# Attention probabilities turned in 32x32 blocks on VectorE and moved by DMA, in place of transposes on TensorE

## The reference

```
# layer 0: graph attention, F1 = 256
h     = x @ W                                   # 512 x 256
e     = leaky_relu(h @ a[0] + (h @ a[1]).T, 0.2)
alpha = softmax(where(adj, e, -1e9))
x     = layernorm(x + concat([alpha @ h, h]))

# layer 1: 8 heads of 64
q, k, v = x @ Wq.T + bq, x @ Wk.T + bk, x @ Wv.T + bv
attn    = softmax(where(adj == 0, -inf, q @ k.T / 8))     # per head, 512 x 512
x       = layernorm(x + (attn @ v) @ Wo.T + bo)
```

## Time and profile before

| | us |
|---|---|
| median of 3 runs | 3468.46 (3467.27 to 3468.61) |
| the profiled execution | 3468.5 |
| its span, first to last instruction | 3466.6 |
| TensorE busy in the span | 3412.3 |
| VectorE busy | 2688.1 |
| ScalarE busy | 2510.2 |
| GpSimd busy | 1616.8 |

### The profile page before, as it was taken

One profiled execution on the slowest core, in us unless ns is written; L12 is line 12 of the kernel. 1 busy time (PEld: TensorE's weight loads), 2 busy tenths in 40 slices (PEclk: granted clock), 3 DMA queues, 4 the chain that ended last, 5 costly groups with the idle time before them and its releaser, 6 DMA issues.

```text
span 3466.6 us, 65791 instructions
## 1 busy us (share of the span) xinstructions
PE 3412.3 (98%) x23168; PEld 2903.8 (84%) x23168; DVE 2688.1 (78%) x7607; ACT 2510.2 (72%) x5382; POOL 1616.8 (47%) x1542
## 2 busy tenths in 40 slices
PE   6999999999999999999999999999999999999998
PEld 5888888888888888888888888888888888888886
DVE  5787777877777877778777778777787777877776
ACT  4776777776777767777777777677777777777775
POOL 2544454445454444544454544445444454444443
PEclk8999999999999999999999999999999999999999
DMA  3000011000111010110001110001100011100100
GB/s 128 19 22 28 25 38 38 31 26 22 34 38 38 20 31 25 37 38 31 26 21 36 38 35 22 26 31 38 38 25 32 19 38 37 32 25 25 31 13 25
DMA packets 59652, 111.19 MB, mean 32 GB/s; under 512 B 6720, under 2 KB 7488, under 8 KB 59328
## 3 DMA queue, kind: packets, MB, share of 16 engines
q1 hardware_dynamic: 59328, 106.99, 9.6%
HBM read 73.41 MB, written 33.55 MB: 31 GB/s over the span
## 4 chain that ended last, share of the span: by engine, by line
PE 97%; DVE 1%; ACT 1%; issue 0%; DMA 0%; POOL 0%; SPq 0%; ACTq 0%; DVEq 0%; POOLq 0%
PE R_bank L541 47%; PE O_bank L629 14%; PE T_bank L613 14%; PE S_bank L603 13%; PE L_bank L541 5%; PE L_bank L532 3%; PE L_bank L556 0%; DMA prob<-WkT 0%; POOL turned L985 0%; DVE prob L900 0%; PE O_bank L541 0%; DMA alpha<-a 0%; ACT tokens L674 0%; DVE n_wide L946 0%; ACT prob L734 0%
## 5 line engine op out<-in xcount | busy, mean ns | idle before, releaser
L965 POOL TENSOR_TENSOR prob<-prob,rsum 128x512 f32<-128x512 f32 x1024 | 1059.5, 1041 | 1309.3 <-DVE rsum L906 1307.4
L734 ACT ACTIVATE prob<-prob,negmax 128x512 f32<-128x512 f32 x1024 | 739.6, 722 | 323.3 <-DVE negmax L900 314.9
L659 ACT ACTIVATE probT<-T_bank 128x512 fp32r<-128x512 f32 x1024 | 579.0, 594 | 220.8 <-PE T_bank L613 214.6
L900 DVE CUSTOM_DVE_ANT_0 prob<-S_bank,mask 128x512 f32<-128x512 f32 x1024 | 695.5, 679 | 2.2 <-PE S_bank L603 1.1
L794 DVE TENSOR_TENSOR probT<-T_bank,probT 128x512 fp32r<-128x512 f32 x1024 | 675.9, 683 | 5.1 <-ACT probT L659 3.1
L613 PE MATMUL T_bank<-ident,prob 128*128 128x128 f32 x4096 | 597.7, 276 | 3.1 <-DVE probT L794 3.1
L629 PE MATMUL O_bank<-probT,v_st 128*128 128x256 f32 x4096 | 586.6, 288 | 2.8 <-DVE probT L794 2.8
L906 DVE RECIPROCAL rsum<-psum_row 128x1 f32<-128x1 f32 x1024 | 164.9, 161 | 542.7 <-PE S_bank L603 303.4
L613 PEld LDWEIGHTS T_bank<-ident,prob 128*128 128x128 f32 x4096 | 459.0, 141 | 106.1 <-issue 93.8
L629 PEld LDWEIGHTS O_bank<-probT,v_st 128*128 128x128 f32 x4096 | 522.2, 190 | 21.5 <-issue 11.5
L603 PE MATMUL S_bank<-qk_pair 64*128 64x512 f32 x3072 | 494.1, 426 | 2.5 <-DVE negmax L900 2.2
(11 more groups left out here) (84 smaller groups left out, 4374.0 us busy)
## 6 DMA issues: line engine op xcount, KB each, us to landing
tokens<-xT SPq DMA_DIRECT2D x128, 256.0 KB, 3.0
tokens<-x SPq DMA_DIRECT2D x128, 256.0 KB, 2.7
out<-tokens SPq DMA_DIRECT2D x128, 256.0 KB, 2.1
tokens<-adj SPq DMA_DIRECT2D x1, 1024.0 KB, 6.5
tokens<-WqT SPq DMA_DIRECT2D x1, 1024.0 KB, 5.5
prob<-WkT SPq DMA_DIRECT2D x1, 1024.0 KB, 7.9
tokens<-WvT SPq DMA_DIRECT2D x1, 1024.0 KB, 6.5
prob<-WoT SPq DMA_DIRECT2D x1, 1024.0 KB, 5.0
```

Of the source, the lines that this page charges most:

```text
L659: act.activation(dst, src, ACT.Copy).then_inc(done, 1)
L734: act.activation(prob[:, slot, :], prob[:, slot, :], ACT.Exp, bias=negmax[:, slot:slot + 1], scale=-1.0, accum_out=psum_row[:, slot:slot + ...
L900: dve.tensor_tensor_reduce(prob[:, slot, :], S_bank[s % 2][:, :], mask[:, s % 8 // 2, :], -SCALE, HUGE, ALU.add, ALU.min, negmax[:, slot:s ...
L965: pool.tensor_tensor(prob[:, slot, :], prob[:, slot, :], rsum[:, slot:slot + 1].to_broadcast([P, N]), ALU.mult).then_inc(p_norm, 1)
```

## The change

The probabilities are no longer transposed on TensorE.

- **Phases.** Four tiles (two row tiles of both heads) are a phase, eight a graph. Tiles 0, 1 and 2 of a phase are normalised on GpSimd (`norm`, now 24 a graph), tile 3 on ScalarE (`anorm`, 8).
- **`vt`** (32 a graph): VectorE's block transpose turns each 32x32 block of a normalised tile of `prob` within itself and writes it to `blocked`, which holds two phases, so that for one block row the pieces of four tiles lie side by side.
- **`mv`** (32 a graph): SyncE moves them, four transfers each, 128 a graph. Each takes 32 partitions of 2 KB to the 32 partitions where they belong in `turned_lo_prob` (two phases). 16 transfers make a phase; the first waits for the phase's fourth turn.
- **`hi` and `lo`**: ScalarE copies a quarter of a phase, 128x512, from `turned_lo_prob` to `turned_hi_prob` (one phase only); GpSimd, not VectorE, subtracts it in place. The first `hi` of a phase waits for both weighs of the phase before.
- **`weigh`** waits for all four `lo` of its phase and reads 256 queries as four runs of 64. `lows` and `sum` put the columns back in order (`by_row_block`).
- **Banks.** The two `T_bank`s go; there are three `S_bank`s, used in turn by tile, and two `L_bank`s. `scores` waits for one tile less to be reduced. N's result is read by ScalarE straight from `L_bank`; `n_wide` and its copy on VectorE go.
- **Buffers.** `turned`, `alpha` and `qk_pair` hold one tile, one tile and one pair where they held two. The reciprocal (`inv`) is a step of its own in VectorE's list.
- All lists of steps are written anew.

The diff, cut:

```diff
+    "scores N k1",
+    "weigh weigh C0",
+    "scores O0 scores",
+    "O1 scores O2",
+    "C1 weigh weigh",
+    "scores O3 q2",
+    "k2 D0 scores",
+    "weigh weigh scores",
+    "C2 D1 W0",
+    "W1 scores W2",
+    "W3 C3 D2",
+    "A3 weigh weigh",
+    "scores D3 q3",
+    "k3 weigh weigh",
+    "E0 E1 scores",
+    "scores V0 V1",
+    "E2 scores E3",
+    "weigh weigh scores",
+    "B0 q4 k4",
+    "B1 weigh weigh",
+    "scores V2 scores",
+    "B2 scores V3",
+    "weigh weigh B3",
+    "q1",
...
+    "norm pair norm",
+    "lo norm lo",
+    "lo lo norm",
+    "norm lo lo",
+    "lo norm lo",
+    "yrs norm norm",
+    "lo lo lo",
+    "norm lo norm",
+    "norm pair lo",
+    "norm lo lo",
+    "lo lrs norm",
+    "norm A0 lo",
+    "lo lo norm",
+    "lo bo0 norm",
+    "norm pair lo",
+    "lo norm A1",
+    "lo lo norm",
+    "norm A2 lo",
+    "lo lo norm",
+    "lo A3 norm",
+    "norm pair lo",
+    "norm lo lo",
+    "lo bo1 bo2",
+    "bo3",
...
+UNITS = {"scores": (16, 3), "reduce": (32, 6), "inv": (32, 5), "exp": (32, 6), "norm": (24, 4), "vt": (32, 4), "mv": (32, 1), "hi": (32, 0), "lo": (32, 0), "weigh": (16, -2), "lows": (8, -1), "sum": (8, -1), "pair": (4, -1), "anorm": (8, 1)}
+ENDING = """weigh weigh sum O0 lows pair evO0 evO1 O1 yst0 yst1 evO2 yst2 fin0 evO3 fin1 fin2 yst3 O2 O3 fin3 yrs"""
...
-        turned = sb("turned", [P, 2, 2, C, P], F32R)
+        turned = sb("turned", [P, 2, C, P], F32R)
...
-        alpha = sb("alpha", [P, 2, N])
+        alpha = sb("alpha", [P, N])
...
-        qk_pair = sb("qk_pair", [P, 2, 4, N], F32R)
+        qk_pair = sb("qk_pair", [P, 4, N], F32R)
...
-        probT = sb("probT", [P, HALVES, 2, T, 2 * P], F32R)
+        blocked = sb("blocked", [P, 2, 4, T, 4, BLK])
+        turned_lo_prob = sb("turned_lo_prob", [P, 2, 4, T, P], F32R)
+        turned_hi_prob = sb("turned_hi_prob", [P, 4, T, P], F32R)
...
-        S_bank = [bank(f"S_bank{i}") for i in range(2)]
-        T_bank = [bank(f"T_bank{i}") for i in range(2)]
+        S_bank = [bank(f"S_bank{i}") for i in range(3)]
         O_bank = bank("O_bank")
         R_bank = [bank(f"R_bank{i}") for i in range(2)]
-        L_bank = bank("L_bank")
+        L_bank = [bank(f"L_bank{i}") for i in range(2)]
...
+        def score_bank(R, s):
+
+            return S_bank[(32 * R.k + s) % 3]
+
+        def moved(R, ph, a):
+
+            return p_moved[ph % 2][a], 64 * ((8 * R.k + ph) // 2 + 1)
+
+        def prob_tile(s):
+
+            return prob[:, s % SLOTS, :]
 
         def o_cols(w):
 
             return slice(2 * P * w, 2 * P * (w + 1))
+
+        def by_row_block(half):
+
+            return half.rearrange("p (t a i) -> p a t i", t=2, a=4)
...
+            def move_probs(R, m):
+                ph, a = m // 4, m % 4
+                if a == 0:
+                    sp.wait_ge(p_turned, R.n(32, 4 * ph + 4))
+                own = slice(BLK * a, BLK * (a + 1))
+                for d in range(4):
+                    sp.dma_start(turned_lo_prob[BLK * d:BLK * (d + 1), ph % 2, a, :, :].rearrange("p c x -> p (c x)").bitcast(F32),
+                                 blocked[own, ph % 2, d, :, :, :].rearrange("p c j i -> p (c j i)")).then_inc(moved(R, ph, a)[0], 16)
...
-                if due(R.n(32, 2 * u)):
-                    pe.wait_ge(s_red, R.n(32, 2 * u))
-                qk = qk_pair[:, pair % 2, :, :]
+                if due(R.n(32, 2 * u - 1)):
+                    pe.wait_ge(s_red, R.n(32, 2 * u - 1))
                 for j, (qp, kp) in enumerate(PARTS):
                     for w in range(2):
                         own, _ = rows_of(w)
-                        last = pe.matmul(S_bank[w][:, :], qk[own, qp, t * P:(t + 1) * P], qk[own, 2 + kp, :],
-                                         start=j == 0, stop=j == 2)
+                        last = pe.matmul(score_bank(R, 2 * u + w)[:, :], qk_pair[own, qp, t * P:(t + 1) * P],
+                                         qk_pair[own, 2 + kp, :], start=j == 0, stop=j == 2)
...
-            def turn_probs(R, s):
-                pe.wait_ge(p_norm, R.n(32, s + 1))
-                if due(R.n(16, s // 2)):
-                    pe.wait_ge(t_lo[s % 2], R.n(16, s // 2))
-                for c in range(T):
-                    last = pe.transpose(T_bank[s % 2][:, c * P:(c + 1) * P], prob[:, s % SLOTS, c * P:(c + 1) * P],
-                                        ident[:, :])
-                last.then_inc(t_mm, 1)
-
             def weigh(R, g):
-                pair, half, w = half_of(g)
-
-                pe.wait_ge(t_lo[w], R.n(16, 4 * pair + 2 * half + 2))
+                ph, w = g // 2, g % 2
+
+                pe.wait_ge(p_lo, R.n(32, 4 * ph + 4))
...
+                    probs = (turned_hi_prob[:, :, c, DH * w:DH * (w + 1)],
+                             turned_lo_prob[:, ph % 2, :, c, DH * w:DH * (w + 1)])[s]
+                    last = pe.matmul(O_bank[:, o_cols(w)], v_st[:, c, (2 * (ph // 2) + w) % HEADS, :], probs,
+                                     start=(c, s) == todo[0], stop=(c, s) == todo[-1])
...
-                if due(R.n(32, 8 * (pair - 1))):
-                    act.wait_ge(s_mm, R.n(32, 8 * (pair - 1)))
+                if due(R.n(32, 8 * pair)):
+                    act.wait_ge(s_mm, R.n(32, 8 * pair))
...
-            def probs_hi(R, s):
-                pair, t, w = tile_of(s)
-                g = 4 * pair + t // 2 * 2 + w
-                if t % 2 == 0 and due(R.n(16, g - HALVES + 1)):
-                    act.wait_ge(pv_mm, R.n(16, g - HALVES + 1))
-                act.wait_ge(t_mm, R.n(32, s + 1))
-                split_hi(probT[:, half_buffer(R, g), HI, :, (t % 2) * P:(t % 2 + 1) * P],
-                         T_bank[s % 2][:, :].rearrange("p (c q) -> p c q", c=T), t_hi)
+            def probs_hi(R, m):
+                ph, a = m // 4, m % 4
+                if a == 0 and due(R.n(16, 2 * ph)):
+                    act.wait_ge(pv_mm, R.n(16, 2 * ph))
+                act.wait_ge(*moved(R, ph, a))
+                split_hi(turned_hi_prob[:, a, :, :], turned_lo_prob[:, ph % 2, a, :, :].bitcast(F32), p_hi)
+
+            def normalise_last(R, ph):
+                slot = (4 * ph + 3) % SLOTS
+                act.wait_ge(p_inv, R.n(32, 4 * ph + 4))
+                act.activation(prob[:, slot, :], prob[:, slot, :], ACT.Copy,
+                               scale=rsum[:, slot:slot + 1]).then_inc(p_norm_act, 1)
...
+                    dve.wait_ge(p_turned, R.n(32, s - SLOTS + 1))
...
-            def probs_lo(R, s):
-                pair, t, w = tile_of(s)
-                buf = half_buffer(R, 4 * pair + t // 2 * 2 + w)
-                dve.wait_ge(t_hi, R.n(32, s + 1))
-                cols = slice((t % 2) * P, (t % 2 + 1) * P)
-                split_lo(probT[:, buf, LO, :, cols], T_bank[s % 2][:, :].rearrange("p (c q) -> p c q", c=T),
-                         probT[:, buf, HI, :, cols], t_lo[w])
+            def turn_blocks(R, s):
+                ph = s // 4
+                if s % 4 == 0 and due(R.n(8, ph - 1)):
+                    for a in range(4):
+                        dve.wait_ge(*moved(R, ph - 2, a))
+                if s % 4 == 3:
+                    if due(R.n(16, 2 * ph - 2)):
+                        dve.wait_ge(pv_mm, R.n(16, 2 * ph - 2))
+                    dve.wait_ge(p_norm_act, R.n(8, ph + 1))
+                else:
+                    dve.wait_ge(p_norm_pool, R.n(24, 3 * ph + s % 4 + 1))
+                dve.transpose(blocked[:, ph % 2, :, :, 2 * (s % 2) + s % 4 // 2, :].rearrange("p d c i -> p c d i"),
+                              prob_tile(s).rearrange("p (c d i) -> p c d i", c=T, i=BLK)).then_inc(p_turned, 1)
...
+            def normalise(R, q):
+                s = q // 3 * 4 + q % 3
                 pool.wait_ge(p_inv, R.n(32, s + 1))
-                slot = s % SLOTS
-                pool.tensor_tensor(prob[:, slot, :], prob[:, slot, :], rsum[:, slot:slot + 1].to_broadcast([P, N]),
-                                   ALU.mult).then_inc(p_norm, 1)
+                pool.tensor_tensor(prob_tile(s), prob_tile(s),
+                                   rsum[:, s % SLOTS:s % SLOTS + 1].to_broadcast([P, N]),
+                                   ALU.mult).then_inc(p_norm_pool, 1)
+
+            def probs_lo(R, m):
+                ph, a = m // 4, m % 4
+                pool.wait_ge(p_hi, R.n(32, m + 1))
+                pool.tensor_tensor(turned_lo_prob[:, ph % 2, a, :, :], turned_lo_prob[:, ph % 2, a, :, :].bitcast(F32),
+                                   turned_hi_prob[:, a, :, :].bitcast(F32), ALU.subtract).then_inc(p_lo, 1)
```

378 lines of the change are left out of this document (165 added, 213 removed).

## The result

| | before | after |
|---|---|---|
| median of four runs each, us | 3468.53 | 3259.26 (3247.06 to 3272.12) |
| the profiled execution, us | 3468.5 | 3247.1 |
| its span, us | 3466.6 | 3245.3 |

The ratio is 0.9397, with a 95% interval of 0.9348 to 0.9447: 6.0% faster. The forecast was 3165 us, 8.7%, in a range from 3080 to 3380. The direction and the range held, but the time lies outside the band that was given most weight (3115 to 3215): 94 us of the gain are missing, and the experiments are about them.

The account below looks back on a forecast made before the run. TensorE was taken to stay the bound, with a floor of 92.7 us a graph, 96.0 with waits; 32 x 96.0 + 91 for ramp and end + 1.9 outside the span = 3165 us, range 3080 to 3380.

Parts of the forecast that it names:

- Part 1: TensorE: without the transposes of the turns, 13.7 us a graph, its floor falls from 106.1 to 92.7 us a graph.
- rival (d): TensorE's floor is lower, toward the busy sum: 92 to 94.5 us a graph with waits, 3080 us; chance 0.06.
- Part 2: Work the other engines take over, per graph: ScalarE 85, GpSimd 84, VectorE 83 us; SyncE 128 moves at 0.46 us each.
- rival (b): VectorE's block turn shares a path with GpSimd: 1.11 us a turn, 100 us a graph with waits, 3293 us; chance 0.12.
- Part 3: The new phase loop of hi, lo and weigh: 94.2 us a graph, 96.0 with the added waits.
- side-by-side scores: Two scores in the fifth gap between weigh pairs; the second waits for the first's tile to be reduced, some 0.7 us.
- hops: Handovers that find ScalarE or GpSimd in the middle of something else: 1 us a graph added.
- Rival (a): The phase loop binds throughout its tight half, each hop meeting a busy engine: 97.5 to 102 us a graph, 3260; chance 0.24.
- rival (c): SyncE becomes the bound at 0.80 us an issue: 107.8 us a graph, 3540 us, slower than now; chance 0.10 with its kin.
- Three score banks at nothing: Scores wait for one reduce less with three banks; costed at nothing, since VectorE at 83 of 96 us keeps up.
- Ramp and end: First graph and last phase outside the steady part: 71.1 us before, 10 us added for each, 91 in all.
- What would show it: Signs in the profile: TensorE near 96% busy, short waits on low part and negmax, turn 0.68 us, GpSimd 84 to 88%.

Follow-up runs that it names:

- the kernel with both edits: The kernel after with two 64-partition moves in place of four of 32, and both alpha passes reading one operand from PSUM: 3105.45 us, ratio 0.8953.

## Why the prediction was right or wrong

| kernel | VectorE's alpha work, us a graph | a graph, us |
|---|---|---|
| slope on ScalarE, one small instruction | 3.6 | 95.7 |
| the same, `aexp` first | 3.6 | 95.6 |
| half as many moves, both passes from PSUM | 5.5 | 93.7 |
| both passes from PSUM | 5.5 | 94.1 |
| the same, 5.5 more behind them | 5.5 + 5.5 | 95.7 |
| mask pass alone from PSUM | 8.2 | 96.4 |
| leaky pass alone from PSUM | 8.2 | 96.4 |
| each PSUM pass twice | 11.0 | 96.7 |
| low part on half the columns | 10.4 | 97.0 |
| slope on ScalarE, two small instructions | 11.0 | 98.5 |
| after | 12.2 | 98.1 |
| half as many moves | 15.7 | 101.3 |

(The middle column is four times the sum of the means of the passes in the stretch. The first two rows do least on VectorE and still aren't the fastest: there ScalarE does the slope, and TensorE waits for alpha or `qk_pair`, as above.)

**Part 1 was right.** TensorE's floor was forecast at 92.7; the kernel with both edits has 93.66 us a graph with TensorE busy 99.0% of it, 92.7. A transpose out of a full TensorE is worth 0.10 us, near the distance of starts that was taken, and rival (d) falls.

**Part 2 was right on what was new and wrong on what was old**, except for SyncE's issues (below). Block turn 0.695 (0.68), high part 0.62, moves landing in 2.0 us (2.1), ScalarE 82.3 us a graph (85), GpSimd 84.7 (83.6). VectorE was forecast at 83.3 and is at 88.4; its alpha passes alone grew from 6.8 (4 times 1.007 and 0.687) to 12.2. The failed step is "VectorE: 83.3 now": it took over the prices of all that stays. The row that rival (b) was built on, a leaky pass with a median of 690 and a longest of 1530 ns, was the row that held the answer. I asked of it only what the new instruction would pay. I should have asked what that old instruction pays when GpSimd goes from 478 to 864 us in 1000. Rival (b) named the right mechanism on the wrong instruction: the turn is untouched at 716 ns at most, the passes pay.
The Trainium skill (SBUF — State Buffer, SBUF: two separate sides) says that the shared port pair is locked for a whole instruction, by GpSimd or by a VectorE instruction with two SBUF inputs, and that whichever starts first gets it. The runs agree on which instructions pay: 681 ns against 1455 by the place of one operand. What they add is who is next: the waiting pass did not always get its turn at the next boundary between GpSimd's instructions, but seven times in the kernel after only when five of them were through, 6.2 us in the timeline above.

**Part 3 came out at the forecast's size for other reasons.** The phase loop followed gave 94.2, of it 1.5 of waits for the low part, and 0.7 for side-by-side scores with 1 for hops made 96.0. With the passes out of the way a graph takes 94.1, but not by that sum: the scores wait 0.90 us for `negmax` once a graph, near the 0.7, while TensorE's waits for the low part are 2.9 us in 1000, 0.3 a graph, and nothing shows the 1 us of hops. The 98.1 of the kernel after are 94.1, plus 3.1 in every graph from passes that are longer (its TensorE waits 0.9 us for alpha and 1.2 for `qk_pair` even in a short graph), plus 0.9 on average from the six graphs that wait out a train and then run at the lower clock for 4 to 7.5 us. Rival (a) had the number, 97.5 to 102, but not the place: TensorE's longest waits are at C, for alpha, not at weigh. So the range held in part by luck: some 2 us of waits a graph that didn't come stood in for half of the 4 us that did.

**SyncE**, rival (c): an issue is 0.59 us, about 0.63 from start to start (14 in 8.8 us), not 0.46. 128 are 81 us of the graph's 98. That is far from the 0.78 from which it would have bound. What it is worth beside the clash no run shows by itself: halving the moves cost 84 us with the clash and gained 17 without it. The rows I took it from were loads over 128 partitions; the moves take 32 partitions of SBUF to 32 others.

**Three score banks at nothing** held, though the reason given, "at 83 of 96 us VectorE keeps up", did not: another 5.5 us on VectorE cost 1.6 to 2.6. What comes late is alpha and `qk_pair`; for `negmax` TensorE waits only at the pair of scores, 11 times in 1000 us.

**Ramp and end** were put at 91, 20 more than before, and are 106.8 (70.4 before). The first store comes 2.3 us earlier than before (224.57 against 226.91), but three graphs at the new pace would have been 24 us shorter: the first rounds gained next to nothing, where I had counted 10 for that. The last graph takes 84.0 us from the store before it to the end of the span, 65.7 before; TensorE waits there up to 7.3 us at a time for a low part, with no other work to put in between. I had 10 for this and it is 18.

In sum, against the profiled execution: 2.1 us a graph too few in the steady part are 66 us, and the ramp 16, together the 82 that lie between 3165 and 3247. The other 12 lie between the profiled execution and the median, and no trace shows them. Had the alpha passes kept their old prices, my hops would have been too high by about as much.

**What would show it**: block turn 0.68 and GpSimd 84 to 88% were right; TensorE near 96% was 95; issues of 0.46 and waits on the low part in the second half of each graph were wrong, waits on `negmax` right but at one place only; the clock of 0.99 in place of 1.00 is that of the stretches behind the long passes (0.97 with half the moves, 1.00 with both passes from PSUM).

**Open**: why a pass gets through after one GpSimd instruction in most cases and after five in others. The trace of the kernel after has both beside the same instructions, a low part, three `bo` and a `norm`. Here is a short case, GpSimd and VectorE, to set beside the long one above:

```profile
1079.92 4.68 POOL L1027 TENSOR_TENSOR tokens<-tokens,bo_wide 128x512 f32<-128x512 f32 x3
```

```profile
1079.44 1.07 DVE L866 SCALAR_TENSOR_TENSOR alpha<-alpha 128x512 f32<-128x512 f32 x1
```

Of the 30 leaky passes that began in that low part, the 23 that began 0.44 to 0.56 us before the first `bo` took 1.03 to 1.14 us, and the seven that began 0.59 to 0.94 us before it took 5.9 to 6.3. So in this kernel it is the moment of the start that decides. But the limit isn't the same everywhere: with half the moves 25 passes that began 1.39 to 1.47 us before the first `bo` all took over 6.7 us, and with the mask pass from PSUM two that began 0.71 and 0.99 us before it got through. All waits of such passes above 2.5 us, in every run, are at these `bo`; the 62 leaky passes that met one low part followed at once by another took 1.2 to 1.7 us. So GpSimd instructions without a pause are not enough for a long wait, and what else it takes is not shown.
The low part on half the columns had no long wait and shorter passes than the kernel after but still 97.0 us a graph, more than the table's other rows let one expect. Its ScalarE and VectorE waited more for moves (32.8 and 23.7 us in 1000, 16.7 and 12.9 in the kernel after), and TensorE's waits of 1.5 to 2.2 us, nearly all for alpha, were followed 14 times by the lower clock, for 55 us in all (40 in the kernel after). What each of the two is worth was not tested. Nor does this kernel show that it was the lighter load on GpSimd that ended the long waits: its pass met the `bo` at another moment, 0.08 to 0.10 us after the first had begun, all 30 times.

## What to carry to other kernels

When a change fills an engine, price again every instruction that shares a path with it, also those that the change doesn't touch: a row whose longest is twice its median is the warning, and its price after depends on how often, and when, it meets the other engine. VectorE instructions with two tensors in SBUF beside a busy GpSimd are worth moving to a PSUM operand or to a per-partition scalar, down to those on one column. And a large share of the chain isn't the price of its removal: relieving the queue that held 34% of it made the kernel 84 us slower, and gained 17 us once the clash was gone.

## What the runs showed of the hardware

- A VectorE pass of 128x512 with both tensor operands in SBUF took 0.69 us alone. In the kernel after it took 1.0 to 1.8 us when it began beside a GpSimd instruction and got its turn behind it, and 5.9 to 6.3 when it waited out five of them; 6.8 is the longest of all runs. With one operand in PSUM neither of the two passes took above 0.69. GpSimd pays too: its subtractions took 1302 ns on average with both passes from PSUM and 1360 with both from SBUF, 1769 at the longest.
- The same wait falls on instructions of one element a partition with two tensors in SBUF: 0.15 us alone, 1.05 and 1.21 in the median, 5.5 at the longest; with a per-partition scalar as the second operand 0.21, always.
- VectorE's transpose in 32x32 blocks of 128x512 float32 takes 0.695 us and is indifferent to GpSimd (661 to 716 ns over 1024).
- A move of 64 KB from 32 partitions to 32 others keeps SyncE for 0.59 us and lands after 2.0; one of 128 KB over 64 partitions keeps it for as long and lands after 2.4.
- ScalarE's Prelu runs at the price of the other functions, 0.715 us for 128x512, in the middle of exponentials and without a table load in the stretch.
- In the kernel after, TensorE's granted clock fell to the lower level, 0.50, for 4 to 7.5 us each of the six times that it had stood idle for 4.5 us; around its waits of 0.9 and 1.2 us it stayed at 1.00.
